# Releasing expert tiles after every group instead of every second one, with re-made instruction orders

## What is computed

```python
x = x + L0_ffn(rigid_transform(x, dx, angle))       # bilinear warp, then two ternary-weight linears with gelu
x = x + L1_ffn(masked_attention_pool(x))            # router, 2 of 4 experts: gelu(x @ w1[e] + b1[e]) @ w2[e]
x = x + L2_ffn(adapter_and_layernorm(x, language))  # one real 256 x 256 matrix stands for the sparse frequency filter
x = x + L3_ffn(x @ W[category] + b[category])       # gate, up and down with ternary weights, silu
```

```python
topk_vals, topk_idx = top_k(xf @ wr + br, 2)        # for each token
gates = softmax(topk_vals)
h = gelu(einsum('nd,edh->enh', xf, w1) + b1)        # 256 -> 1024, four experts
y = einsum('enh,ehd->end', h, w2) + b2              # 1024 -> 256
# of y, the two chosen experts' rows are combined with the gates
```

## Time and profile before

| | |
|---|---|
| median of three runs | 2167.25 us |
| the profiled execution | 2157.03 us, of which the span is 2154.9 us |
| PE busy | 1925.3 us, 89% of the span |
| DVE busy | 1741.6 us, 81% |
| ACT busy | 1475.0 us, 68% |
| POOL busy | 1032.0 us, 48% |

### The profile page before, as it was taken

One profiled execution on the slowest core, in us unless ns is written; L12 is line 12 of the kernel. 1 busy time (PEld: TensorE's weight loads), 2 busy tenths in 40 slices (PEclk: granted clock), 3 DMA queues, 4 the chain that ended last, 5 costly groups with the idle time before them and its releaser, 6 DMA issues.

```text
span 2154.9 us, 43565 instructions
## 1 busy us (share of the span) xinstructions
PE 1925.3 (89%) x11400; PEld 1499.2 (70%) x11400; DVE 1741.6 (81%) x8027; ACT 1475.0 (68%) x2591; POOL 1032.0 (48%) x1092
## 2 busy tenths in 40 slices
PE   1445798899999999999999999999999999999986
PEld 1122476678787777878787777787778777887653
DVE  5998988999898898999899989999986555434685
ACT  1145566667867787876588788888778776566654
POOL 1665656766456655566755555645632212111230
PEclk9655699899999999999999999999999999999998
DMA  6246566555657656655555665657576456554560
GB/s 225 90 132 193 185 184 182 177 156 165 184 159 231 200 150 187 180 140 162 162 164 156 200 192 170 180 168 213 142 237 185 144 173 199 158 178 157 171 196 26
DMA packets 310624, 369.17 MB, mean 171 GB/s; under 512 B 127042, under 2 KB 257511, under 8 KB 298988
## 3 DMA queue, kind: packets, MB, share of 16 engines
q1 hardware_dynamic: 279376, 290.73, 45.0%
q0 software_dynamic: 28672, 68.21, 11.3%
q10 hardware_dynamic: 2332, 7.46, 0.9%
HBM read 277.06 MB, written 80.79 MB: 166 GB/s over the span
## 4 chain that ended last, share of the span: by engine, by line
PE 38%; DVE 5%; DMA 4%; POOL 4%; issue 3%; SPq 2%; ACT 1%; DVEq 0%; ACTq 0%; POOLq 0%
PE bank L1708 10%; PE bank L1724 10%; PE bank L1600 4%; PE bank L1606 3%; PE bank L1588 2%; PE bank L1777 2%; PE bank L1798 2%; POOL w_win L1333 2%; PE bank L1594 1%; DMA w_win<-in_windows,w_idx 1%; PE bank L1759 1%; PE bank L1766 1%; DMA moe_y_back<-moe_out_sorted,rows_back 1%; POOL moe_in_sorted L1351 1%; PE bank L1693 1%
## 5 line engine op out<-in xcount | busy, mean ns | idle before, releaser
L1333 POOL DMA_INDIRECT w_win<-in_windows,w_idx x512 | 543.1, 1061 | 445.4 <-DMA w_win<-in_windows,w_idx 174.5
L1708 PE MATMUL bank<-moe_xT,moe_w_tile 128*128 128x256 f32 (+1 forms) x2624 | 574.5, 363 | 5.4 <-ACT moe_xT L1492 3.6
L1724 PE MATMUL bank<-moe_w,moe_hidden_T 128*128 x2336 | 565.5, 383 | 5.3 <-ACT moe_hidden_T L1509 3.0
L1708 PEld LDWEIGHTS bank<-moe_xT,moe_w_tile 128*128 128x128 f32 x2624 | 457.5, 193 | 71.1 <-issue 9.8
L925 DVE TENSOR_TENSOR w_prod<-w_win,w_hat 128x36 f32<-128x36 f32 x4096 | 492.8, 214 | 17.4 <-issue 12.1
L1724 PEld LDWEIGHTS bank<-moe_w,moe_hidden_T 128*128 128x128 f32 x2336 | 427.8, 191 | 67.0 <-issue 13.8
L1509 ACT ACTIVATE moe_hidden_T<-bank,moe_b 128x256 f32<-128x256 f32 (+1 forms) x656 | 257.8, 446 | 164.4 <-PE bank L1708 159.3
L1365 POOL DMA_INDIRECT moe_y_back<-moe_out_sorted,rows_back x128 | 130.8, 1022 | 272.3 <-DVE rows_back L1177 166.7
L1351 POOL DMA_INDIRECT moe_in_sorted<-c,rows x128 | 142.8, 1115 | 104.3 <-issue 46.5
L1509 ACT ACT_TABLE_LOAD x102 | 130.9, 1283 | 34.7 <-PE bank L1708 32.9
L1251 DVE SCALAR_TENSOR_TENSOR hidden_back<-bank,back_stats,hidden_back 128x512 f32<-128x512 f32 x112 | 83.2, 743 | 70.0 <-ACT hidden_back L1550 69.3
(11 more groups left out here) (306 smaller groups left out, 3689.2 us busy)
## 6 DMA issues: line engine op xcount, KB each, us to landing
moe_w_tile<-in_moe_w SPq DMA_DIRECT2D x82, 1024.0 KB
L_cond_W<-in_L_cond_W SPq DMA_DIRECT2D x112, 256.0 KB
adapters<-in_adapter SPq DMA_DIRECT2D x128, 192.5 KB
moe_out_sorted<-zero_row SPq DMA_DIRECT2D x18, 1024.0 KB
gamma_beta<-in_gamma_beta SPq DMA_DIRECT2D x128, 128.0 KB
moe_x<-moe_in_sorted SPq DMA_DIRECT2D x64, 256.0 KB
moe_out_sorted<-moe_y SPq DMA_DIRECT2D x64, 256.0 KB
x_front<-in_x SPq DMA_DIRECT2D x32, 256.0 KB
```

Of the source, the lines that this page charges most:

```text
L1333: gp.indirect_dma_start(out=V[:, g_ * WLEN:(g_ + 1) * WLEN], out_offset=None, in_=t["windows"], in_offset=bass.IndirectOffsetOnAxis(ap=idx ...
L1708: last = te.matmul((H0, H1)[r % 2][:, (f % FPU) * TILE:(f % FPU) * TILE + width(n)], W1[n % 3][:, d * F + f * P:d * F + (f + 1) * P], XT[: ...
L1724: last = te.matmul(Y[:, u * D:(u + 1) * D], hT[:, (f % (2 * FPU)) * TILE + u * P:(f % (2 * FPU)) * TILE + (u + 1) * P], ap(moe2, weight + ...
```

## The change

`STRIDE` goes, and `RELEASES` lists how many groups each plan of each block takes. In every block the first plan still takes two groups, and each later one takes one. The blocks and the tiles are the same. A block of eight now releases 1, 2, 2, 2, 2, 2 and 8 tiles, a block of four 1, 2 and 8. There are 26 plans instead of 16.

```diff
-SUPERS = (2,4,8,8,6,4)
-STRIDE = 2
+RELEASES = ((2,),(2,1,1),(2,1,1,1,1,1,1),(2,1,1,1,1,1,1),(2,1,1,1,1),(2,1,1))
+SUPERS = tuple(sum(r) for r in RELEASES)
...
-        for first in range(0, n, STRIDE):
-            groups = min(STRIDE, n - first)
+        for r, groups in enumerate(RELEASES[c]):
+            first = sum(RELEASES[c][:r])
```

All five strings of `ORDER` are new. Four keep the number of their letters; DVE's has 3771 instead of 3641, and the 130 more are `p`, 13 for each added plan. One line of it before and now:

```diff
-        "iiicciiiiwiiwwiwiwiwiwwiiwwiwiwiwiwiiwwwiwiwiwiwiiwwwiwiwiwiwiwwwwwwwwcwwwwfwfwfwfwiwfwwwwwiiwwiwiwfwwwfwwfwfwfw"
...
+        "iiicciiiiwiiwwiwiwiwiwwiiwwiwiwiwiwiiwwwiwiwiwiwiiwwwiwiwiwiwiwwwwwwwwcwwwwfwfwfwfwiwfwwwwwwiiwwwiwifwwwfwwfwfwfw"
...
```

More of the change, by code:

```diff
@@ L260 @@
[L260 to L267 removed]
+        "iiicciiiiwiiwwiwiwiwiwwiiwwiwiwiwiwiiwwwiwiwiwiwiiwwwiwiwiwiwiwwwwwwwwcwwwwfwfwfwffwiwwwwwwiiwwwiwifwwwfwwfwfwfw"
@@ new lines @@
+    "scalar":
+        "iihhhhihhhhfhhfffhhffffffahhafafafaaahhffffffahafhafafaaahfffhfffaafhhaffaaafeafffhhefeafeafhheeafeeafeafeaeaffh"
+        "feheffeaehaefheaefeafeehhafefaafefeeeffeeaehafeeheefeaefaehheafefaafefefefeahehfaebabfeeafehhaeaafffefbefflbaeba"
+        "feaefeahheeflaehhleaaffelbffeeffellaehhafeleeflealelfeahhlfeaeffaafehhffeeeefeleleeaelheefaeleeleeleellfelaeeaff"
+        "fheafaaeffhhebebaefafeaeefhheaeffabfefaahlffehaalbeflbaeelafehaheelaalefelfelfelfhlbfeheffelaeahlfheleafeleafebl"
+        "lbafelaaffeflheelffhelaebafhehaelfeafeaalafelffbflbefleelafeaflhheellfelbfaehfheaflfeffafalealeelfheahlleeafelae"
+        "lelfaheelfhfafeaafehffeheeahefaheafeeeafeahffaafehfeffeeehfeheeeaeefaeeefeaeeffefahfehaeaaffehheeafaeeabefebafee"
+        "hhafeafafebfffelbaebaflhhlaeelbeaflelafeelaaelffeflhflehlffehhalealbfeelbaefleelafbelhfleaffleaaflheflfahhafelal"
+        "beelbafeleelafelbaafellffelfhhlfefeaebalhblefaleheblelafeleafelalahhelffflefeffehlhelbaelbeaflelaelbeelaflehlfea"
+        "hlaafehffhfeelebfflbelafeallbeflaelelafhlehlafefaafhfhelelebffelbeaeleelfaelebellfleeflaeehhefleaflfeaflaaeelfle"
+        "fleaflhhlealefabeebfahheeffafeaabfelffhhbebaalfelbaleealelfeleelafelaahlheflfffehhfleflbblaeafleelabelfleelafell"
+        "afefaaffelffelbablfallaelbeellaflfealaafefeflfelbffelbaelflaelebaellafleflefffeleflbafelbelleleeblleaalleelelebe"
+        "lbealeleealeelblealeelaeeelelaebaaeleblelelbelleeleleelelbelbellelbelleeleleelelbelbelleelbellelleeelelbelbellee"
+        "lbellelleeelelbeleeelbeleeleellebletebbettbtlttbtbtltltlblltlbblltlttbtlttbbttltllbltllbblltlttbtlttbbttltllbltl"
+        "llltltttttttt",
@@ new lines @@
+    "sync":
+        "xxggmiigirrgrrrgrcgrrzzzorgrmbbxgrrzzzzzzzorrgmgrrxborrtlmwwgxlwgrrorlwrmgywxlgrryzzzowrlrgymwlgrrxywlyzzzgorlrw"
+        "ywmlgryrxlyorrgtwwmlgrrxybwoylrrgmwlcgrxyrwlgoyrrwlgryrmwlxsgbbyorlwrcywgrlrywlgywylsmbxlyorrwgrwlrmybgxoclyrrmw"
+        "grrxlwyglyswbbzzzorgclwrrmygrxlyzorswwgrbbmlyrgxcrylorrtlwwgrysrmbbwgxlycorrwlgrrymwlsgxbyowlrgrryrmlwgxywlorygr"
+        "wlrrywlygmwlyxgorrrlyrwmwlxbygorcgrlyrmwrwlgxysbbclwygorrrrmlwgyxsobblcygmwrrrlwryxgsbblycgortwrmlwrrgyxwyslbbcw"
+        "gorlrrrygmwlysxgbbclworryrrgwlmysxbbclwgoyrlwgryrrwlsybbmcxylwgorrrylrswbmglwbxygocrrrylmwrwlxysbbcoylrrrrtwmwly"
+        "sxbbcwoqrrlyrmrsbxblwcyowlmysbblwcyowlysbbwclywlywlsybbcylwtwlysbblwcywlysbblwcywlysbblwcywlysbbblwcylybysbqybbc"
+        "bvbqsbbcbvbqbsvsv",
```

136 lines of the change are left out of this document (58 added, 78 removed).

## The result

| | kernel before | changed kernel |
|---|---|---|
| median of 20 runs each, same chip | 2162.57 us | 2156.51 us |
| lowest and highest | 2155.13, 2174.77 | 2148.04, 2164.39 |
| the profiled execution, its span | 2157.03, 2154.9 | 2162.59, 2160.8 |
| ratio, with its 95% interval | | 0.9969, 0.9954 to 0.9983 |

The changed kernel is 6 us faster, 0.3%, well within the 1% that the prediction calls no change. The forecast of 2157 us is met. So the two traces differ by +5.9 us where the kernels differ by -6.1, and about 12 us of any difference between them is scatter of single executions.

What follows compares the result with a forecast made beforehand. PE was taken to bound 466 to 2021 us, DVE the start. From the profiled 2157.0 us, -14 + 4 = -10 gives 2147; for the median, 2167.25, the forecast is 2157, range 2133 to 2181.

Steps and rivals of the forecast that it cites:

- two main terms: 14 us won at the hole near 400 us, and 4 us lost to added plans in 466 to 1600 us.
- (a): Whole kernel: same tiles, widths and matmuls, so no PE work is added or removed.
- (b): Hole, 341 to 422 us: tiles released a group earlier fill PE's gap; 14 us won, between 8.4 and 21.5.
- the 0.9 asked for: Sign of being right: PE's granted clock share from 382 to 422 us rises above 0.9.
- (c): Ten more plans on DVE, eight weighing in 466 to 1600 us: 4 us lost, between 0 and 22.
- the 25 to 35 named: Sign of being right: PE's idle time in the long middle lies between 25 and 35 us.
- (d): Final plans shrink from ten tiles to eight, their 80-element steps to 64: nothing to speak of.
- (e): First tiles of releases: SP waits for scatters ten times more; 0, covered by over 40 us of PE work.
- (f): Tail behind the last tile: same steps in the same order for groups 26 to 31, so 0.
- DVE as the bound: Rival, chance 0.12: eight plans are not absorbed and bring stalls; 26 us slower, 2193 us.
- the hole stays: Rival, chance 0.10: the two tiles come late or the front moves; nothing won, about 2173 us.
- More than the hole: Rival, chance 0.22: all 21.5 us won, plus half the combine and layer norm waits; 30 us faster, 2137 us.

Runs made afterwards that it cites:

- early: Kernel before with the changed kernel's order and releases only up to 470 us: 2292.03 us, 1.0001 of before on the same chip; repeated, 1.0045.
- late_2: Repeat of late on another chip (order of before up to 440 us, then the changed kernel's): 2391.21 us, 1.0263 of the kernel before.
- after_again: The changed kernel itself, measured again on another chip: 2362.67 us, 1.0082 of the kernel before there.
- tax_heavy: As tax, with 117 more unread small VectorE instructions in each of the ten added plans: 2375.44 us, 1.0201 of the kernel before.
- tax: Kernel before with only the ten added plans' VectorE steps and SyncE's scatter waits put in: 2292.67 us, 0.9952 of before; repeated, 1.0023.
- late: Order of the kernel before up to 440 us, then the changed kernel's order and releases: 2345.16 us, 1.0215 of the kernel before.
- spread: As early, but the rest's expert steps moved ahead by 20 us at 470, falling to 0 at 1400: 2417.66 us, 1.0373 of the kernel before.

## Why the prediction was right

The number was right, and by the balance of the traces its two main terms are near: 11.7 won at the hole for 14, and 6.0 lost in the middle for 4. A third, the tail, was put at nothing and is not. That 2157 was hit within 1 us is luck on top: the forecast was -10 from a median of 2167.25, while the change is -6.1 (-10 to -3.7 by the interval) from a median of 2162.57 over 20 runs, so the gain was taken 4 us too large and the base 4.7 too high, and the two errors cancel. And the experiments show that the two main terms are not the separate things that the prediction added up.

- **(a), the same PE work:** right. 11400 matmul records in both.
- **(b), the hole:** right in place and way. The plan and the tiles came in time, the expert steps fill 391 to 419 us, and the clock share of 382 to 422 rose from 0.74 to 0.91, just over the 0.9 asked for. Loss in 341 to 422 fell by 11.7 where I took 14. Counted from the fifth to the ninth routing block, as the prediction asked, it fell by 11 us, 23.0 to 11.8 (the two rows below this list: 12.7 + 0.06 x 172 and 7.9 + 0.02 x 197). The low clock that is left, 6.8 us at 0.50, lies from 382 to 389 us, where PE had just been idle for the 2.73 us ahead of 383.01.
- **Where the step was thin:** "everywhere but in the hole that is worth nothing by itself, it only moves work" is true, but I did not ask what the work leaves behind. `early` gives back all of its 12.8 us within 100 us. On the first chip the changed kernel keeps its gain, presumably by an order made anew as a whole; DVE is about as full as before there, 183.44 of the 197 us in which it routes groups 5 to 8 against 158.32 of 172 (the same two rows). On the other chips it gives most of it back. `late_2` against `after_again`, 22 us or more, would put the hole at the upper end of my 8.4 to 21.5, if it were the hole's worth alone, which the loss there (9.5 us) doesn't bear out.

- **(c), the plans' tax:** the load is right: DVE's busy time rose by 18.3 us (14 to 28 forecast), 1.8 a plan, inside 1.4 to 2.77. Its price, scaled by DVE's slack, was 4; by the 0.47 of `tax_heavy` eight plans of 1.8 would cost 7, and `tax`, which has them all, shows 0 within some 7. The middle's idle time is 31.2, within the 25 to 35 named. So 4 was fair. What I left out is that the order around the plans changes too: `late` is over 2% slower where plans and borders together can't explain it. If the hole were worth 22 us on the first chip as well, the rest would cost 22 - 6 = 16 us there and not 4; the traces of that chip show 6.0 of it in the middle and some 4 in the tail, so that stays a possibility and not a result.
- **(d) and (e)** at nothing: SyncE's ten more waits show up as one late tile (1.3 us).
- **(f), the tail** at nothing: wrong. The prediction says that the tail has the same steps in the same order. But PE's string has 96 letters behind its last `e` before and 101 now, and they alternate differently. It costs some 4 us of loss, as large as the tax, in every trace whose strings end like this.
- **The rivals:** DVE as the bound is out by `tax`. That the hole stays is out by the trace of the first chip, though the front did move, by 16 us at group 5 and 20 at group 6. "More than the hole" did not come: the waits for the combine and the layer norm did shrink, and others took their place.

The fifth to the ninth routing block, in the changed kernel and in the kernel before:

```profile
352.00:549.00 197.00, 189.13 (x1110) 153.87 (x1109) 183.44 (x983) 140.15 (x270) 123.85 (x130) 0.98 0.60 180
```

```profile
341.00:513.00 172.00, 159.31 (x898) 124.95 (x897) 158.32 (x856) 110.23 (x229) 115.23 (x119) 0.94 0.62 180
```

**Open:** why the changed kernel's order behind 440 us is the slower one on the other chips. It is not the plans, and the borders explain little; the tail is 4 to 5 us of it. `spread` makes the spacing of expert steps to front steps the suspect, but no run moved that alone within the changed kernel. How much of `early` and `late` is the price of their seams is open too: a run that joins the same two orders at another place would tell. Nor could `early`, `late` and `tax` be repeated on a chip like the first.

## What to carry to other kernels

Filling a hole in one engine's time with work from behind it only moves the hole, unless the stretch that gives the work up can run faster or is refilled in turn: ask of every us moved ahead what is missing where it came from. When two parts of a change are priced one by one in orders written for each other, test them by taking each out of the whole (`late`) as well as by putting each in alone (`early`); here the one says 22 us or more and the other 0. Such mixtures have a seam, which needs a test of its own. A stretch that is taken to be unchanged is checked in the instruction order, and then in more than one trace: here a tail that was priced at nothing costs some 4 us each time. And a difference of under 1% in a kernel with five in-order engines should be measured on more than one chip before it is believed in either direction.

## What the hardware showed that I had not expected

On the four chips of the experiments the kernel before takes 6 to 8% longer than in the first measurement, though the instructions themselves take as long. One line of DVE, 466 to 1600 us, in the kernel before on the first chip and in `after_again`:

```profile
L925 DVE TENSOR_TENSOR w_prod<-w_win,w_hat 128x36 f32<-128x36 f32 x2816 | 339.7, 214 | 5.0 <-ACT w_hat L1420 2.1 <-DMA w_win<-in_windows,w_idx 2.1
```

```profile
L926 DVE TENSOR_TENSOR w_prod<-w_win,w_hat 128x36 f32<-128x36 f32 x2432 | 297.9, 215 | 17.5 <-issue 15.7 <-DVE router_logits L1036 1.0 <-DVE w_cols L938 0.4
```

214 and 215 ns a piece. The time is lost between instructions: PE is idle 2373.8 - 1992.0 = 382 us of `after_again`, 242 of the changed kernel on the first chip. It goes in stops that take several engines at once. Around one of them, in order of start:

```profile
469.17 0.40 PE L1589 MATMUL bank<-ident_f,q_front 128*128 128x128 f16 x4
...
470.12 1.99 PE L1709 MATMUL bank<-moe_xT,moe_w_tile 128*128 128x256 f32 x8
...
477.98 0.60 ACT L1484 ACTIVATE q1T_front<-bank 128x512 bf16<-128x512 f16 x1 [9.20 <-remote]
...
478.63 1.03 PE L1601 MATMUL bank<-L_w_ternary,q1T_front 128*128 128x512 fp8e4 x2 [6.52 <-issue]
...
480.19 0.42 DVE L1007 TENSOR_TENSOR xT_front<-bank,mask 128x256 f32<-128x256 f32 x1 [10.26 <-remote]
```

ACT's L1484 needs PE's L1589, which has ended by 469.57; the semaphore step that L1589 carries is recorded at 477.96, 8.4 us later, and ACT starts at once. GpSimd's gathers go on all the while, up to 478.09. Counting such times behind 440 us, over 0.3 us long, in which PE, ACT and DVE are idle together: one in each of the two traces of the first chip (1.9 and 0.4 us), 56 in `after_again` (69 us), 22 in `tax` (29 us). DMA is not slower: the packets of the main queue take 45.0% of 2155 us before and 42.4% of 2290 in `tax`. What holds the engines up, no run here tells, nor whether it belongs to the chip or to the time of the measurement. Each stop can cost more than itself: in the 4 us behind 29 of the 56 the mean granted clock is under 0.75, and that of the whole span is 0.916 against 0.946.
